# A graph attention layer on one core: the score bound from eight late tiles, exponentials straight from h, a third bank for h, and a new written order

## The reference, cut to what matters

```
h = relu(layernorm(x))                                  # x: 4096 x 256
h = h @ W.T                                             # W: 256 x 256
e = leaky_relu((h @ a1)[:, None] + (h @ a2)[None, :], 0.2)
e = where(adj == 0, -9e15, e)                           # adj: 4096 x 4096, int32
out = x + softmax(e, axis=1) @ h
```

## Time and profile before

| | |
|---|---|
| median of three runs | 384.48 us |
| the profiled execution: its own time | 384.67 us |
| the profiled execution: span from first to last instruction | 382.9 us |
| matmuls (PE) busy | 376.8 us, 98% |
| weight loads (PEld) busy | 330.7 us, 86% |
| VectorE (DVE) busy | 363.9 us, 95% |
| ScalarE (ACT) busy | 195.1 us, 51% |
| GpSimd (POOL) busy | 42.0 us, 11% |

### The profile page before, as it was taken

The page is one execution under the profiler, slowest core; times in us unless marked ns, Lnnn a source line. Parts: engine busy times, 40 slices in busy tenths (PEclk is TensorE's granted clock), DMA queues, the critical chain, the costliest instruction groups (busy, mean ns, idle before and its releaser), DMA issues.

```text
span 382.9 us, 9216 instructions
## 1 busy us (share of the span) xinstructions
PE 376.8 (98%) x3358; PEld 330.7 (86%) x3358; DVE 363.9 (95%) x458; ACT 195.1 (51%) x271; POOL 42.0 (11%) x66
## 2 busy tenths in 40 slices
PE   8999899999999999999999999999999999999996
PEld 6788688888888888888888888888888888888885
DVE  4999999999999999999999999999987999999965
ACT  5899754744443644344445544444446443444330
POOL 3897020000000001110000002100000012100000
PEclk9999999999999999999999999999999999999999
DMA  7922476847676666776676667766665577766503
GB/s 241 370 78 56 130 235 218 287 154 238 217 236 208 205 220 214 243 229 218 220 223 207 209 217 233 236 222 225 215 205 184 168 222 240 232 220 221 165 2 110
DMA packets 27024, 78.22 MB, mean 204 GB/s; under 512 B 3956, under 2 KB 9336, under 8 KB 27000
## 3 DMA queue, kind: packets, MB, share of 16 engines
q1 hardware_dynamic: 25712, 74.72, 60.9%
q0 software_dynamic: 1280, 3.16, 2.2%
q10 hardware_dynamic: 8, 0.00, 0.0%
HBM read 73.66 MB, written 4.21 MB: 203 GB/s over the span
## 4 chain that ended last, share of the span: by engine, by line
PE 96%; ACT 1%; DVE 1%; DMA 1%; issue 1%; ACTq 0%
PE ps L1390 87%; PE ps L1214 2%; PE ps L1229 2%; PE ps L1235 2%; PE ps L1240 2%; DMA a_rows<-a 1%; PE ps L1179 1%; PE ps L1195 1%; DVE rows_sb L1119 0%; ACT c_row L494 0%; ACT h_sb L468 0%; ACT L620 0%; ACT p_hi L504 0%; ACTq L479 0%; DVE inv_den L1115 0%
## 5 line engine op out<-in xcount | busy, mean ns | idle before, releaser
L1390 PE MATMUL ps<-v_sb,p_hi 128*128 (+2 forms) x2048 | 251.8, 273 | 1.0 <-ACT p_hi L504 0.9
L514 ACT ACTIVATE p_hi<-p_sb,gp 128x1024 f16<-128x1024 f32 x126 | 144.4, 1149 | 166.6 <-DVE p_sb L785 140.0
L1390 PEld LDWEIGHTS ps<-v_sb,p_hi 128*128 128x128 f16 x2048 | 199.6, 98 | 26.9 <-issue 1.2
L792 DVE SCALAR_TENSOR_TENSOR p_lo<-p_sb,gp,p_hi 128x1024 f16<-128x1024 f32 x126 | 160.8, 1277 | 7.1 <-ACT p_hi L514 6.7
L785 DVE SCALAR_TENSOR_TENSOR p_sb<-c_row,gp,adj_sb 128x1024 f32<-128x1024 uint32 (+1 forms) x126 | 160.5, 1278 | 0.0
L1390 PE MATMUL ps<-v_sb,p_lo 128*128 (+1 forms) x1024 | 142.7, 273 | 0.0
L1390 PEld LDWEIGHTS ps<-v_sb,p_lo 128*128 128x128 f16 x1024 | 100.0, 98 | 12.7 <-DVE p_lo L792 0.2
L452 POOL DMA_DIRECT2D out<-rows_sb x24 | 13.0, 541 | 263.1 <-DVE rows_sb L1086 262.9
L401 POOL TENSOR_SCALAR hn_sb<-x_sb,moments,rstd 128x256 f32<-128x256 f32 x17 | 21.3, 1261 | 4.3 <-DVE rstd L734 3.4
L744 DVE SCALAR_TENSOR_TENSOR hnt_lo<-ps,hnt_hi 128x256 f16<-128x256 f32 x32 | 12.9, 410 | 0.5 <-ACT hnt_hi L484 0.5
L1229 PE MATMUL ps<-w_hi,hnt_hi 128*128 128x258 f16 x64 | 12.5, 277 | 0.5 <-ACT h_sb L468 0.4
(11 more groups left out here) (85 smaller groups left out, 87.3 us busy)
## 6 DMA issues: line engine op xcount, KB each, us to landing
adj_sb<-adj_t SPq DMA_DIRECT2D x128, 512.0 KB, 4.8
x_sb<-x SPq DMA_DIRECT2D x7, 512.0 KB, 8.3
out<-rows_sb POOLq DMA_DIRECT2D x24, 128.0 KB, 4.3
c_row<-c_flat SPq DMA_DIRECT2D x3, 512.0 KB, 6.1
out<-rows_sb SPq DMA_DIRECT2D x8, 128.0 KB, 1.7
x_sb<-x SPq DMA_DIRECT2D x2, 256.0 KB, 3.8
c_row<-s_flat SPq DMA_DIRECT2D x1, 512.0 KB, 3.8
w_nat<-w SPq DMA_DIRECT2D x1, 256.0 KB, 2.8
```

The costliest lines, as they stand in the source:

```text
L514: nc.scalar.activation(p_hi[:, u % R, :], p_sb[:, u % R, :], ACT.Copy, scale=p_scale[:, bass.ds(t, 1)])\
L792: nc.vector.scalar_tensor_tensor(out=p_lo[:, u % R, :], in0=p_sb[:, u % R, :], scalar=p_scale[:, bass.ds(t, 1)], in1=p_hi[:, u % R, :], op ...
L1390: return nc.tensor.matmul(ps[:, k, 0:width], part[:, u % R, k * P:(k + 1) * P], v_sb[:, bass.ds(t, 1), v, 0:width], start=start, stop=stop ...
```

## The change

- The bound D takes the last eight tiles, in two halves of four (SPREAD), from the high parts of their turned rows; d from h_sb is needed for tiles 0 to 23 alone. There are two spreads and two reductions to d_top, and one more small step that joins the first with d_early (d_so_far).
- g and p_scale are computed by ScalarE directly from d in h_sb, with scale and bias as operands, as two exponentials (`exp_p`, `exp_g`) in place of one; VectorE's four gp_args steps go, and one small step (p_bias) comes.
- h has three banks instead of two; turned tiles have three instead of four.
- The written order of every engine is laid out anew, with other tiles normalised by other engines and other pairs of values split by other engines. In this, `warm` moves from the start of ScalarE's list to between source tiles 28 and 29 of the first group, `table_ready` from before the first exponential to between source tiles 20 and 21, and the second half of w_hi, which the first projection waits for, behind the high parts of tiles 0 and 1.
- On GpSimd the scales for the exponentials move from the start to behind its last normalised tile.

The diff, cut to its core:

```diff
-    LATE = 4
+    LATE = 8
+    SPREAD = 4
...
-    BY_VECTOR = [26]
-    BY_SCALAR = [0, 1] + list(range(4, 14, 2)) + [15, 19, 21, 23, 24, 25, 29]
-    BY_GPSIMD = [2] + list(range(3, 15, 2)) + [14, 16, 17, 18, 20, 22, 27, 28, 30, 31]
+    BY_VECTOR = [24, 25]
+    BY_SCALAR = [1, 4, 8, 10, 13, 14, 17, 18, 20, 23, 26, 28]
+    BY_GPSIMD = [0, 2, 3, 5, 6, 7, 9, 11, 12, 15, 16, 19, 21, 22, 27, 29, 30, 31]
...
-        bank_w, bank_n, bank_d, bank_e = 4, 1, 4, 5
-        bank_h = 6
-        banks_t = (2, 3, 1, 0)
+        bank_w, bank_n, bank_d, bank_e = 4, 1, 5, 0
+        banks_h = (6, 7, 4)
+        HB = len(banks_h)
+        banks_t = (2, 3, 1)
...
-            def exp_gp(tiles, n):
-                act.wait_ge(gp_args_ready, n)
-                nc.scalar.activation(gp[:, :, tiles], gp_args[:, :, tiles], ACT.Exp).then_inc(gp_ready, 1)
+            def exp_g(t0, t1):
+                act.wait_ge(c_bias_ready, 1)
+                act.wait_ge(h_kept, t1)
+                nc.scalar.activation(g_col[:, t0:t1], h_sb[:, t0:t1, F + 1], ACT.Exp,
+                                     bias=exp_bias[:, 0:1], scale=exp_scale[:, 1:2]).then_inc(g_ready, 1)
+
+            def exp_p(t0, t1):
+                act.wait_ge(p_bias_ready, 1)
+                act.wait_ge(h_kept, t1)
+                nc.scalar.activation(p_scale[:, t0:t1], h_sb[:, t0:t1, F + 1], ACT.Exp,
+                                     bias=p_bias[:, 0:1], scale=exp_scale[:, 3:4]).then_inc(p_scale_ready, 1)
...
-            act.wait_ge(consts_ready, 2)
-            nc.scalar.activation(warm[:], eps_sb[:], ACT.Sqrt)
             act.wait_ge(w_nat_loaded, 16)
...
+            def top_of(m):
+                dve.wait_ge(d_spread, m + 1)
+                nc.vector.tensor_reduce(d_top[:, m:m + 1], ps[:, bank_d, 0:SPREAD * P], AX.X, ALU.max).then_inc(d_top_ready, 1)
...
+            top_of(0)
+            split_hn_lo(29)
             dve.wait_ge(d_turned, 1)
             nc.vector.tensor_reduce(d_early[:], ps[:, bank_e, 0:P], AX.X, ALU.max).then_inc(d_early_ready, 1)
+            value_lo(4)
             dve.wait_ge(d_top_ready, 1)
             dve.wait_ge(d_early_ready, 1)
-            nc.vector.tensor_scalar(d_safe[:], d_top[:], d_early[:, 0:1], D_MARGIN, ALU.max, ALU.add).then_inc(d_safe_ready, 1)
-            dve.wait_ge(scales_ready, 5)
+            nc.vector.tensor_scalar(d_so_far[:], d_top[:, 0:1], d_early[:, 0:1], None, ALU.max).then_inc(d_so_far_ready, 1)
+            top_of(1)
+            dve.wait_ge(d_top_ready, 2)
+            dve.wait_ge(d_so_far_ready, 1)
+            nc.vector.tensor_scalar(d_safe[:], d_top[:, 1:2], d_so_far[:, 0:1], D_MARGIN, ALU.max, ALU.add).then_inc(d_safe_ready, 1)
+            dve.wait_ge(scales_ready, 6)
             dve.wait_ge(d_safe_ready, 1)
             nc.vector.tensor_scalar(exp_bias[:], d_safe[:], exp_scale[:, 2:3], None, ALU.mult).then_inc(c_bias_ready, 1)
+            split_hn_lo(30)
             dve.wait_ge(c_bias_ready, 1)
-            nc.vector.tensor_scalar(gp_args[:, 0, 0:R], h_sb[:, 0:R, F + 1], exp_scale[:, 1:2],
-                                    exp_bias[:, 0:1], ALU.mult, ALU.add).then_inc(g_args_ready, 1)
-            dve.wait_ge(g_args_ready, 1)
-            nc.vector.tensor_scalar(gp_args[:, 1, 0:R], gp_args[:, 0, 0:R], 0.25, math.log(P_UP), ALU.mult, ALU.add)\
-                .then_inc(gp_args_ready, 1)
-            value_lo(10)
+            nc.vector.tensor_scalar(p_bias[:], exp_bias[:], 0.25, math.log(P_UP), ALU.mult, ALU.add).then_inc(p_bias_ready, 1)
+            value_lo(6)
             weights_part(0, 0)
+            split_hn_lo(31)
...
             def project_hi(t):
                 pe.wait_ge(hnt_hi_ready, t + 1)
-                if t >= 2:
-                    pe.wait_ge(*kept(t - 2))
+                if t >= HB:
+                    pe.wait_ge(*kept(t - HB))
...
-                        if t == 0 and k == bank_h:
-                            pe.wait_ge(*kept(T - 2))
-                        if t == 0 and k == bank_h + 1:
-                            pe.wait_ge(*kept(T - 1))
+                        if t == 0 and k in banks_h:
+                            pe.wait_ge(*kept(max(i for i in range(T) if banks_h[i % HB] == k)))
```

More of the change, by code:

```diff
@@ L406, in value_hi @@
                 nc.gpsimd.tensor_copy(v_sb[:, t:t + 2, 0, 0:F], h_sb[:, t:t + 2, 0:F]).then_inc(v_hi_gpsimd, 1)
+            normalise(0)
+            normalise(2)
+            normalise(3)
+            normalise(5)
+            normalise(6)
+            normalise(7)
+            normalise(9)
+            pool.wait_ge(wa_hi_ready, 1)
+            nc.gpsimd.tensor_copy(w2_hi[:], w_hi[:, :, F + 1:FW].to_broadcast([P, KC, P])).then_inc(w2_ready, 1)
+            value_hi(0)
+            normalise(11)
+            value_hi(2)
+            normalise(12)
+            normalise(15)
+            normalise(16)
+            normalise(19)
+            normalise(21)
+            normalise(22)
+            value_hi(4)
+            value_hi(6)
+            normalise(27)
+            normalise(29)
+            normalise(30)
+            normalise(31)
             pool.wait_ge(norms_ready, 1)
@@ L746, in split_hn_lo, with split_w_lo @@
                     .then_inc(hnt_lo_ready, 1)
+            def split_w_lo(c):
+                dve.wait_ge(wa_hi_ready, 1)
+                dve.wait_ge(w_hi_ready, c + 1)
+                nc.vector.scalar_tensor_tensor(out=in_halves(w_lo)[:, c], in0=w_in_psum[:, c], scalar=w_scale[:, 0:1],
+                                               in1=in_halves(w_hi)[:, c], op0=ALU.mult, op1=ALU.subtract)\
+                    .then_inc(w_lo_ready, 1)
             def normalise(t):
@@ L814, in _ @@
             gather(3)
-            dve.wait_ge(wa_hi_ready, 1)
-            for c in range(KC):
-                dve.wait_ge(w_hi_ready, c + 1)
-                nc.vector.scalar_tensor_tensor(out=in_halves(w_lo)[:, c], in0=w_in_psum[:, c], scalar=w_scale[:, 0:1],
-                                               in1=in_halves(w_hi)[:, c], op0=ALU.mult, op1=ALU.subtract)\
-                    .then_inc(w_lo_ready, 1)
-            rstd_of(1)
-            stats_of(4)
-            stats_of(5)
+            split_w_lo(0)
             dve.wait_ge(wa_scale_ready, 1)
@@ L1038, in _ @@
             edge_weights(6, 22, 96, 0)
+            value_lo(22)
             split_lo(5, 21, 16)
+            split_lo(6, 22, 16)
             dve.wait_ge(p_lo_ready, 20)
@@ L1060, in _ @@
             split_lo(3, 27, 24)
+            value_lo(28)
             dve.wait_ge(p_lo_ready, 26)
@@ L1067, in _ @@
             split_lo(5, 29, 24)
+            value_lo(30)
             dve.wait_ge(p_lo_ready, 28)
@@ L1290, in _ @@
             project_lo(7)
-            turn(9)
             turn(10)
```

449 lines of the change are left out of this document (212 added, 237 removed).

## The result

The changed kernel took **390.95 us**, the median of 5 runs (390.82 to 392.81). The kernel before took 384.48 us beside it (384.35 to 384.56, 5 runs). The ratio is 1.0181, with a 95% interval of 1.0161 to 1.0201: 6.5 us slower. The range of the prediction ended at 386.9 us. The profiled execution of after took 390.95 us with a span of 389.0 us, against 384.67 and 382.9 us before.

A forecast was written before the change was run, and what follows sets the result against it. TensorE was taken to bound the kernel, so only its start of products could move. An earlier second spread, six tiles, products and 2.6 us of holes gave +0.6 us: 385.1 us, range 384.1 to 386.9.

The forecast's parts named there:

- The start: Norms and w_hi's second half late, first projection 0.7 to 0.8 us late; 0 lasting cost, ends -0.3 and +0.8.
- Rival (a): Start: TensorE's clock rises later after idling, 0 to 3.2 us lost, 1.6 taken; total 386.3 us; chance 0.18.
- The middle: Last batch to second spread: tile 31 turned at 34.0, spread ends at 35.5 us, 1.0 earlier than before.
- The bound: After the second spread: exp_bias ready about 1.6 us later; GpSimd's scales covered with 0.3 to spare.
- The table load: Behind keep_h of tile 26: c starts 3.0 us after the second spread, leaving a 2.1 us hole at tile 30's pair.
- Rival (b): A table switch costs more than its load where the next function is waited for: +0.6 + 1.8, 386.9 us; chance 0.03.
- After that: First group: two more value_lo cost VectorE 1.3 us, gained back at 2.4 a tile against TensorE's 2.64.
- rival (d): VectorE falls behind in the first group, with more work and less lead: +1.3 us on top, 386.4 us; chance 0.08.
- The load between tiles 28 and 29: Moved dummies draw one more 1.28 us load where ScalarE idles: costs nothing, 1.5 us if the idle time were gone.
- The sum: First low product at 44.3 us against 43.75 before, later holes included: +0.6 us.

The follow-up runs named there:

- Run 2: Changed kernel with only VectorE's step for the last columns of w_lo moved later, behind w_lo's second half; w_hi's second half stays late: 387.65 us.
- run 8: Kernel before with one line moved: ScalarE forms the second half of w_hi behind the split of tile 1: 389.04 us, ratio 1.012.
- Run 3: Changed kernel with filler matmuls in TensorE's two idle stretches at the start, all waits left as they are: 390.26 us, ratio 1.0149.
- Run 1: Changed kernel with the second half of w_hi made directly behind the first, as before the change: 386.58 us, ratio 1.005.
- Run 4: Changed kernel with the dummy exponential, and so its table load, moved ahead to in front of h of tile 24: 390.17 us, ratio 1.0154.
- run 6: Changed kernel with w_hi's second half early, value_hi of tiles 8 to 11 on GpSimd and their value_lo before VectorE's first weights: 385.71 us.
- run 5: Changed kernel with both w_hi's second half right behind the first and the exp table load in front of keep_h(24): 385.22 us, ratio 1.0022.

## Why the prediction was wrong

**The start, the step that failed.** Its details held: the norms at 5.98 (6.05 was forecast), the end of w_hi at 10.12 (10.3), the first projection 0.77 us late (0.7 to 0.8; in order of time it starts at 10.21, and before at 9.44). Its conclusion was wrong: "I take 0 for TensorE and VectorE once the next tiles are reached, with ends of -0.3 and +0.8". I followed the moved step to the engine that I thought of, TensorE, and asked when the first projection would run. I did not ask who else waits for w_hi. VectorE does (L845), and with it everything that its list has behind that step. Run 2's trace shows that the projection's delay was indeed worth 0 there, and run 8 that the moved line alone costs 4.5 us. The measured price of the step, put at 0, is 2.87 us at the three tiles and 4.17 us at the last batch, with the standstill. Why lateness grows by 1.30 us there stays open.

**Rival (a), TensorE's clock**, named the right engine state and not the right course. It had the clock rise later, because of the idle time in front of the first projection, and gave "between 0 and 3.2 us lost", 1.6 taken. That idle time alone did nothing in run 2 (0.89 us, clock 1.00 behind it). In after the clock was at its upper level when the pair that the chain has at 12.35 us took 0.22, and then fell, behind the second idle stretch of 1.31 us that VectorE's wait had made. Run 3 puts 1.57 us on it; that this is the 1.6 taken, the middle of a range for another course, is luck. The loss came on top of the wait, not in its place, and the slack of 0.8 us in the middle covered nothing, since VectorE was late too. The Trainium skill (TensorE: Matmul & The Clock Gate, Part 1) says that the clock follows how busy the array has just been; the windows above agree with it (0.68 and 0.50 behind the idle stretch, 1.00 with fillers in it).

**The middle was right, once the start is set right.** Run 1 is the kernel that this part described:

```profile
28.35 0.19 DVE L749 RECIPROCAL rstd<-std 128x8 f32<-128x8 f32 x1
28.64 5.08 POOL L405 TENSOR_SCALAR hn_sb<-x_sb,moments,rstd 128x256 f32<-128x256 f32 x4 [0.37 <-DVE rstd L749]
```
The inverse was forecast at 28.4, tile 31 normalised at 28.7 + 5.3 = 34.0; it is 28.64 + 5.08 = 33.7. The second spread was to end at S = 35.5 and ended at 35.26 (34.83 + 0.43, as the rows of after at 38.90 and 39.33 show for its length). In after S is 39.33, which is 35.5 plus the 3.8 that the start had cost by then.

**The bound** was right in size (exp_bias 1.5 behind S) and not quite in its cover: exp_bias waits 0.19 us for the scales, where I had 0.3 to spare.

**The table load** came where it was forecast, with c at S + 3.0 in after (42.33 - 39.33) and in run 1 alike. Tile 30's pair was owed at S + 2.64 = 41.97 and started at 44.40: a hole of 2.43, forecast 2.1. The 0.3 between them are p and g: from 42.84 to 43.40 they hold ScalarE for 0.56 us, where I had 0.25. Run 4's trace prices the exposed load at 1.18 us. The drain that the Trainium skill (ScalarE: Activation LUTs, What ACT_TABLE_LOAD costs) puts on top of the load does not show here either: the load ends at 42.32 and c starts at 42.33. Rival (b) is out by the same row.

**After that**: the forecast that VectorE gains back the two more value_lo of the first group ("it needs 2.4 a tile against TensorE's 2.64 and gains that back") was wrong, and **rival (d)** was right, also on top. VectorE begins the group behind and gains, with the more value steps among its tiles, too little until 129 us. The price was given as 1.3; it is 1.15 in after and 1.14 in run 2 (81.23 - 80.09), and run 6, without the two, takes it to 0.06 (80.15 - 80.09).

**The load between tiles 28 and 29** cost nothing, as forecast: it stands at 119.81 us, ScalarE's next high part still waits 0.33 us for VectorE behind it, and so does the next product that waits at all (0.34 us, at 129.64).

**The sum.** The forecast was +0.6 us. To it come 4.17 for the start and the standstill and 0.3 for the longer hole, 0.24 goes off for the second spread (35.26 in run 1 for 35.5), and about 1.4 comes for the first group, whose sum had counted 0.3 of later holes in before alone: 0.6 + 4.17 + 0.3 - 0.24 + 1.4 = 6.2, for 6.13 measured. Rivals (a) and (d) stood beside the forecast as cases of their own; both were true at once, and with them the wait that no case named.

## What to carry to other kernels

When a step moves back on one engine, list every wait on its semaphore on all engines, and for each waiting step read what stands behind it in its queue: here a step of 0.2 us that nobody needed soon held back the one that everybody needed. Rivals that feed one another (a wait, the clock that falls in it, less lead for the engine behind) are one case with one chance, not three. An early gain of TensorE is worth nothing where another engine paces the next stage: run 5's first low product was 0.6 us early and its last stretch 0.56 late.
